# The layer norm of layer 1 by row tiles inside the feed-forward's tail, and modulation columns from one-column products

## What is computed

```
mod = (silu(c) @ wmod).reshape(1, 6, 1, 512)       # wmod is 512 x 3072
sa, ca, ga, sb, cb, gb = mod parts 0..5
g = (2 * (g >= 0) - 1) * maximum(abs(g), 0.25)      # for ga and gb
h = layernorm(x) * (1 + ca) + sa
x = x + ga * attention(h)
h = layernorm(x) * (1 + cb) + sb
x = x + gb * ffn(h)
```

## Time and profile before

| | |
|---|---|
| median of three runs | 1811.9 us |
| the profiled execution | 1815.9 us, its span 1814.0 us |
| busy in the span | PE 92%, its weight loads 74%, DVE 66%, ACT 56%, POOL 40% |
| mean granted clock of TensorE | 0.958 |
| norm 1 and feed-forward of layer 0 | about 979 to 1236 us |
| norm 2 and QKV of layer 1 | about 1236 to 1316 us |
| output of layer 1's attention, norm 3 | about 1681 to 1753 us |

### The profile page before, as it was taken

One profiled execution on the slowest core, in us unless ns is written; L12 is line 12 of the kernel. 1 busy time (PEld: TensorE's weight loads), 2 busy tenths in 40 slices (PEclk: granted clock), 3 DMA queues, 4 the chain that ended last, 5 costly groups with the idle time before them and its releaser, 6 DMA issues. The chain is left out here.

```text
span 1814.0 us, 28444 instructions
## 1 busy us (share of the span) xinstructions
PE 1675.2 (92%) x10115; PEld 1344.5 (74%) x10115; DVE 1192.8 (66%) x2924; ACT 1008.7 (56%) x2229; POOL 724.9 (40%) x656
## 2 busy tenths in 40 slices
PE   4899999999999999999997799996779999999778
PEld 2698999999999999899885588784645555554557
DVE  5667777677677777777667533355876777773475
ACT  2477777777877777777773211102216666666131
POOL 3286675756747567485531200000532222211200
PEclk8999999999999999999999899997959999999889
DMA  7101000000010100100003112005000000000021
GB/s 187 37 13 30 19 24 26 23 30 18 25 36 13 30 19 24 30 13 24 18 7 88 67 53 65 2 1 184 1 1 1 1 1 1 1 1 1 30 45 47
DMA packets 72358, 56.07 MB, mean 31 GB/s; under 512 B 23023, under 2 KB 54447, under 8 KB 72219
## 3 DMA queue, kind: packets, MB, share of 16 engines
q1 hardware_dynamic: 70634, 53.47, 10.2%
q10 hardware_dynamic: 1584, 0.79, 0.2%
HBM read 52.14 MB, written 2.10 MB: 30 GB/s over the span
## 5 line engine op out<-in xcount | busy, mean ns | idle before, releaser
L746 PEld LDWEIGHTS psum<-a_probsT,a_v 128*128 128x128 f32 x2304 | 294.7, 191 | 25.6 <-issue 3.9
L746 PE MATMUL psum<-a_probsT,a_v 128*128 128x128 f32 x2304 | 299.2, 275 | 1.7 <-ACT a_probsT L956 1.6
L845 DVE CUSTOM_DVE_ANT_0 psum<-psum,a_keys_allowed 128x128 f32<-128x128 f32 (+7 forms) x256 | 195.7, 764 | 83.0 <-PE psum L77 74.4
L939 ACT ACTIVATE a_probs<-psum,a_neg_max 128x128 f32<-128x128 f32 (+7 forms) x256 | 190.7, 745 | 66.6 <-DVE a_neg_max L845 58.2
L1827 ACT ACTIVATE a_probsT<-psum 128x512 f32<-128x512 f32 (+3 forms) x384 | 174.6, 497 | 86.4 <-PE psum L1664 62.4
L948 ACT ACTIVATE a_probs<-a_probs,a_row_inv 128x128 f32<-128x128 f32 (+7 forms) x256 | 201.1, 786 | 27.9 <-DVE a_row_inv L852 27.7
L609 POOL TENSOR_TENSOR a_turned_pool<-a_q_sum,a_sine 64x512 f32<-64x512 f32 x62 | 79.3, 1278 | 287.8 <-DVE a_q_sum L831 286.6
L875 DVE TENSOR_TENSOR a_ctxT_lo<-psum,a_ctxT_hi 128x128 fp32r<-128x128 f32 x256 | 73.7, 288 | 172.7 <-ACT a_ctxT_hi L962 172.6
L956 ACT COPY a_probsT<-psum 128x512 f32<-128x512 f32 (+3 forms) x384 | 173.2, 488 | 18.7 <-PE psum L734 16.6
L865 DVE SCALAR_TENSOR_TENSOR a_sumT<-psum,a_scale_o,a_sumT 128x512 f32<-128x512 f32 x248 | 173.6, 742 | 0.9 <-PE psum L760 0.7
L734 PE MATMUL psum<-ident,a_probs 128*128 128x128 f32 x1152 | 168.9, 274 | 0.7 <-ACT a_vT L933 0.5
(11 more groups left out here) (348 smaller groups left out, 3963.7 us busy)
## 6 DMA issues: line engine op xcount, KB each, us to landing
a_raw_o<-in_L_attn_qw_o SPq DMA_DIRECT2D x32, 256.0 KB, 2.8
a_raw_q<-in_L_attn_qw_q SPq DMA_DIRECT2D x31, 256.0 KB, 3.3
mod1b_w<-in_L_wmod SPq DMA_DIRECT2D x4, 1024.0 KB, 11.3
mod0a_w<-in_L_wmod SPq DMA_DIRECT2D x3, 1024.0 KB, 13.0
mod0b_w<-in_L_wmod SPq DMA_DIRECT2D x3, 1024.0 KB, 7.0
f_raw<-in_L_ffn_down_w SPq DMA_DIRECT2D x10, 256.0 KB, 3.1
f_raw<-in_L_ffn_gate_w SPq DMA_DIRECT2D x10, 256.0 KB, 3.3
f_raw<-in_L_ffn_up_w SPq DMA_DIRECT2D x10, 256.0 KB, 3.6
```

What stands on the lines that cost most here:

```text
L746: last = nc.tensor.matmul(bank(use)[:, 0:P], v[:, g % 2, j, :], probsT[:, u % 2, j, :], start=(j == 0), stop=(j == i))
L845: nc.vector.tensor_tensor_reduce(out=scores, in0=scores, in1=keys_allowed[:, S - (i + 1) * P:S], scale=-1.0, scalar=-MASKED, op0=ALU.add, ...
L939: nc.scalar.activation(probs[:, u % 3, 0:(i + 1) * P], score[u % 2][:, 0:(i + 1) * P], ACT.Exp, bias=neg_max[:, h % 2, i:i + 1], scale=-1. ...
```

## The change

It has four parts.

1. **One-column products.** A modulation column is made straight: the stationary is a 128 by 128 block of wmod, the streamed operand one column of silu(c); four blocks of k add into one PSUM column, and 32 such products give two parts. DVE then only copies four numbers per partition and adds 1 to the scale. The diagonals are gone. `silu_rows` is needed only for gate rows; ACT makes it now.
2. **Layer 1's first columns in norm 1.** The two parts of wmod that norm 2 used are loaded in norm 1's block behind the first weight tiles. PE makes their columns at that block's end, DVE takes them.
3. **Norm 2 by row tiles in the feed-forward's tail.** The class `RowNorm` does the whole norm for a single tile: DVE begins (statistics), ACT takes the root, DVE finishes, PE turns four blocks, ACT applies scale and shift in place in PSUM and casts, DVE makes the low part. Its steps stand between those of the down product. The cast of the hidden tile goes from DVE to ACT. Tiles 6 and 7 are completed in the QKV block.
4. **w_qkv in the tail.** It is loaded in four blocks of columns (384 KB each, in pieces of 512 bytes), turned behind the down products of tiles 2 to 5, cast by ACT, and its low part made by DVE. The QKV block begins with its products at once; the bias and the table of the rotation are the first loads in it. Places in on-chip memory are assigned by hand so that all this fits beside the feed-forward.

The core of the diff:

```diff
-    def make_columns(self, pe, pair, silu_rows, rows_used):
-
-        pe.wait_ge(self.mem.modulation["rows_done"], KT * rows_used)
+    def make_columns(self, pe, pair):
+
         for c, n in enumerate(pair):
-            last = self.multiply(pe, n, silu_rows, self.mem.bank[4 + c])
+            pe.wait_ge(self.mem.modulation[f"w_in{n}"], 16 * (self.layer + 1))
+            for piece in range(KT):
+                for k in range(KT):
+                    last = self.nc.tensor.matmul(self.mem.bank[4 + c][:, piece:piece + 1],
+                                                 self.w[:, self.parts.index(n), k, piece * P:(piece + 1) * P],
+                                                 self.mem.silu_c[:, self.layer, k:k + 1], start=(k == 0), stop=(k == KT - 1))
         last.then_inc(self.mem.modulation["column_made"], 1)
 
-    def take_columns(self, dve, pair, diagonals):
+    def take_columns(self, dve, pair):
 
         at = 4 * self.layer + (0 if pair[0] == 0 else 2)
-        number = self.number(pair[0])
-        dve.wait_ge(self.mem.modulation["column_made"], number)
-        for c in range(2):
-            for k in range(KT):
-                self.nc.vector.scalar_tensor_tensor(
-                    out=diagonals[c][:, k * P:(k + 1) * P], in0=self.mem.bank[4 + c][:, k * P:(k + 1) * P], scalar=1.0,
-                    in1=self.mem.ident[:, :], op0=ALU.mult, op1=ALU.mult,
-                    accum_out=self.mem.column[:, at + c, k:k + 1]).then_inc(self.mem.modulation["diagonals"], 1)
-        dve.wait_ge(self.mem.modulation["diagonals"], 2 * KT * number)
-        self.nc.vector.tensor_scalar(self.mem.column[:, at + 1, :], self.mem.column[:, at + 1, :], 1.0, None, ALU.add
+        dve.wait_ge(self.mem.modulation["column_made"], self.number(pair[0]))
+        self.nc.vector.tensor_copy(self.mem.column[:, at, :], self.mem.bank[4][:, 0:KT])
+        self.nc.vector.tensor_scalar(self.mem.column[:, at + 1, :], self.mem.bank[5][:, 0:KT], 1.0, None, ALU.add
...
+            if next_columns:
+                next_columns.take_columns(dve, (0, 1))
 
...
+            if next_columns:
+                modulation.wait_columns(pe, pair)
+                next_columns.make_columns(pe, (0, 1))
...
+    def begin(self, dve, t):
+        nc, sem = self.nc, self.by_dve.sem
+        nc.vector.bn_stats(self.stats[:, t, :], self.mem.x[:, t, :]).then_inc(sem, 1)
+        dve.wait_ge(*self.by_dve.of(("stats", t)))
+        nc.vector.bn_aggr(self.mean_var[:, t, :], self.stats[:, t, :]).then_inc(sem, 1)
+        dve.wait_ge(*self.by_dve.of(("moments", t)))
+        nc.vector.tensor_scalar(self.y[:, t, :], self.mean_var[:, t, 1:2], LN_EPS, None, ALU.add).then_inc(sem, 1)
+
+    def finish(self, dve, t):
+        nc, sem, of = self.nc, self.by_dve.sem, self.by_dve.of
+        root, newton = self.root[:, t, :], self.newton[:, t, :]
+        dve.wait_ge(*self.by_act.of(("std", t)))
+        nc.vector.reciprocal(root, self.std[:, t, :]).then_inc(sem, 1)
+        dve.wait_ge(*of(("root", t)))
+        nc.vector.tensor_tensor(newton, root, root, ALU.mult).then_inc(sem, 1)
+        dve.wait_ge(*of(("square", t)))
+        nc.vector.tensor_tensor(newton, newton, self.y[:, t, :], ALU.mult).then_inc(sem, 1)
+        dve.wait_ge(*of(("product", t)))
+        nc.vector.tensor_scalar(newton, newton, -0.5, 1.5, ALU.mult, ALU.add).then_inc(sem, 1)
+        dve.wait_ge(*of(("newton", t)))
+        nc.vector.tensor_tensor(self.rstd[:, t, :], root, newton, ALU.mult).then_inc(sem, 1)
+        dve.wait_ge(*of(("rstd", t)))
+        if t >= 2:
+            dve.wait_ge(*self.turned.of(t - 2))
+        nc.vector.tensor_scalar(self.normed[:, t % 2, :], self.mem.x[:, t, :], self.mean_var[:, t, 0:1], self.rstd[:, t, :],
+                                ALU.subtract, ALU.mult).then_inc(sem, 1)
+
+    def low(self, dve, t):
+        dve.wait_ge(*self.by_act.of(("high", t)))
+        cols = self.columns(t)
+        self.nc.vector.tensor_tensor(self.mem.hT[1][:, :, cols], self.banks[t % 2].rearrange("p (k n) -> p k n", k=KT),
+                                     self.mem.hT[0][:, :, cols].bitcast(F32), ALU.subtract).then_inc(self.by_dve.sem, 1)
+
...
+    def modulate(self, act, t):
+        act.wait_ge(*self.turned.of(t))
+        bank = self.banks[t % 2]
+        for k in range(KT):
+            piece = bank[:, k * P:(k + 1) * P]
+            last = self.nc.scalar.activation(piece, piece, ACT.Identity, scale=self.scale[:, k:k + 1], bias=self.shift[:, k:k + 1])
+        last.then_inc(self.by_act.sem, 1)
+        act.wait_ge(*self.by_act.of(("h", t)))
+        self.nc.scalar.copy(self.mem.hT[0][:, :, self.columns(t)], bank.rearrange("p (k n) -> p k n", k=KT)
+                            ).then_inc(self.by_act.sem, 1)
+
+    def turn(self, pe, t):
+        pe.wait_ge(*self.by_dve.of(("normed", t)))
+        if t >= 2:
+            pe.wait_ge(*self.by_dve.of(("low", t - 2)))
+        for k in range(KT):
+            last = self.nc.tensor.transpose(self.banks[t % 2][:, k * P:(k + 1) * P], self.normed[:, t % 2, k * P:(k + 1) * P],
+                                            self.mem.ident[:, :])
+        last.then_inc(self.turned.sem, 1)
...
+                if 1 <= t < NT - 1:
+                    norm.turn(pe, t - 1)
+                if 0 <= t - NEXT_FIRST < KT:
+                    turn_next(t - NEXT_FIRST)
...
+            act.wait_ge(*hidden_done.now(LAST, "up"))
+            for t in range(1, NT):
+                if t + 1 < NT:
+                    cast(t + 1)
+                if t >= 2:
+                    norm.modulate(act, t - 2)
+                if 0 <= t - 1 - NEXT_FIRST < KT:
+                    take_next(t - 1 - NEXT_FIRST)
+                norm.deviation(act, t - 1)
...
-            for t in range(NT):
+                dve.wait_ge(added, t + 1)
+
+            def split_next(k):
+                dve.wait_ge(next_hi, k + 1)
+                nc.vector.tensor_tensor(next_wT[1][:, k, :], next_bank, next_wT[0][:, k, :].bitcast(F32), ALU.subtract
+                                        ).then_inc(next_split, 1)
+
+            for t in range(2):
+                split(t, slice(LAST, NF), t + 3)
+            for t in range(1, NT):
+                add(t - 1)
+                if t + 1 < NT:
+                    low_part(t + 1)
+                norm.begin(dve, t - 1)
                 if t >= 2:
-                    dve.wait_ge(produced, t - 1)
-                split(t, slice(LAST, NF) if t < 2 else slice(0, NF), t + 3)
-                if t:
-                    add(t - 1)
-            add(NT - 1)
-
-
-def layer1_qkv_phase(nc, mem, q1, k1, v1, rope_dram, w_dram, b_dram, wmod, late):
+                    norm.low(dve, t - 2)
+                norm.finish(dve, t - 1)
+                if 0 <= t - 1 - NEXT_FIRST < KT:
+                    split_next(t - 1 - NEXT_FIRST)
...
+            norm.turn(pe, NT - 2)
             for t in range(NT):
+                if t == 1:
...
+            dve.wait_ge(produced, NT)
+            nc.vector.tensor_tensor(mem.x[:, NT - 1, :], mem.bank[(NT - 1) % 2][:, :], mem.x[:, NT - 1, :], ALU.add).then_inc(added, 1)
+            dve.wait_ge(added, NT)
+            norm.begin(dve, NT - 1)
+            norm.low(dve, NT - 2)
+            norm.finish(dve, NT - 1)
```

More of the change, by code:

```diff
@@ L1011, in layer0_ffn_phase @@
+def layer0_ffn_phase(nc, mem, w, wmod, wmod_next, w_qkv):
     slots, kts, tiles, halves, matrices = range(2), range(KT), range(NF), range(NHALF), (2, 0, 1)
@@ L1085, in stack_low, with loads_of_next @@
                                    ALU.subtract).then_inc(low_step, 1)
+        def loads_of_next(sp):
+            loads(sp)
+            for n in (0, 1):
+                next_modulation.load(sp, n)
         with ExitStack() as first:
@@ L1196, in _, with turn_next @@
                 project(f, 1, 1)
+            def turn_next(k):
+                pe.wait_ge(next_in[k % 2], 16 * (k // 2 + 1))
+                if k:
+                    pe.wait_ge(next_split, k)
+                for c in range(NC):
+                    last = nc.tensor.transpose(next_bank[:, c * P:(c + 1) * P], next_raw[:, k % 2, c, :], mem.ident[:, :])
+                last.then_inc(next_turned, 1)
             for t in range(NT):
@@ L1338, in loads @@
                 late.load(sp, n)
-        with ExitStack() as first:
-            modulation = Modulation(nc, mem, first, "mod1a", 1, (0, 1), wmod)
-            layernorm_phase(nc, mem, 2, loads, modulation)
-        wT = (sb("wT_hi", [P, KT, QKV1], F32R), sb("wT_lo", [P, KT, QKV1], F32R))
-        qkv = sb("qkv", [P, 2, QKV1])
-        part = [sb(f"part{n}", [P, NH, NP]) for n in range(4)]
-        roped = sb("roped", [P, 2, NH, HD1])
-        wT_turned, w_hi, w_split = sem("wT_turned"), sem("w_hi"), sem("w_split")
-        projected, biased, v_out = sem("projected"), sem("biased"), sem("v_out")
-        turned = {"even": sem("even_turned"), "odd": sem("odd_turned")}
-        summed = {"even": sem("even_summed"), "odd": sem("odd_summed")}
```

(6 more changed lines are left out.)

242 lines of the change are left out of this document (154 added, 88 removed).

## The result

The changed kernel takes 1791.96 us (median of four, 1791.2 to 1792.77) against 1811.91 (1811.73 to 1813.33): ratio 0.9889, 95% interval 0.9872 to 0.9906. Its profiled execution took 1791.9 us, span 1789.8, against 1815.9 and 1814.0: 24.2 us less. The profiled execution before lay 4.0 us above its median, this one lies on it, so some 4 of the 24.2 belong to the executions and not to the change. Timed again beside the kernel before, it was 23.0 us faster (1789.73 against 1812.77).

The account below looks back on a forecast made before the run. PE was taken to bound the feed-forward's tail, a chain the hand-over, and DVE the QKV stage and last norm. -28.9+5.5+2.1 = -21.3 us gave 1790.6 on the median, forecast 1791 us, range 1778 to 1800.

Parts of the forecast that it names:

- A: Feed-forward tail and hand-over to QKV: layer-norm block and w_qkv turning leave the path, transposes join PE's tail; -28.9 us.
- the low part ahead of the second QKV tile: QKV stage: DVE's low part of tile 7 (0.69 us) goes where 0.46 us was idle; 0.5 us back.
- B: Norm before the feed-forward: one-column products and layer 1's columns make it longer; +5.5 us, bounds +2.3 and +8.8.
- C: Last norm (run 3): DVE loses silu copies and diagonals, but columns and gate row come later; +2.1 us, bounds -2.1 and +6.6.
- the middle between full and half clock: Last norm: columns ready at 1736.3 at full clock, 1742.8 at half; 1739.5 was taken.
- Nothing: Norm of run 0 and the output phase's silu rows: no effect, since ACT is held until 31.09 by weight loads.
- 1 (full clock): Rival: one-column products run at full clock since PE counts as busy; -31.5 in all, 1780 us, chance 0.28.
- PE counts as busy: Reason given for full clock in the one-column products: PE counts as busy, so the clock rises.
- the statement on transposes: Skill page, used for the clock in the norm before the feed-forward: transposes don't lift the clock as products do.
- 2 (0.46 us a record): Rival: one-column products adding into one PSUM column wait for each other, 0.46 us a record; +45, 1857 us, chance 0.06.
- 3: Rival: DVE bounds the tail, its round 9.6 instead of 7.5 us, PE waits before six products; 1797 us, chance 0.10.
- 4: Rival: the small bias and rope loads land late, first QKV tile starts at 1250; +4, 1795 us, chance 0.11.

Follow-up runs that it names:

- second profile: The changed kernel timed and profiled again with no edit, on the chip of the follow-up runs: 1789.73 us.
- 32 bytes further: The changed kernel with every hand-placed tensor of the feed-forward moved 32 bytes further, nothing else: 1795.32 us.
- 32 columns: The changed kernel with every column product streaming 32 equal columns of silu(c) instead of one: 1792.65 us.
- address sweep: The changed kernel with 216 unused products added ahead of the tail, their operands starting at different addresses: 1847.29 us in one execution.

## Why the prediction was right, point by point

**A, the hand-over: right, but for one step.** Forecast -28.9, measured -34.2+3.8+0.8 = -29.6. Its terms: block change, four transposes, one product and the way to VectorE come to 5.4 us behind the last product's end, as forecast. The transposes cost 0.115 (groups of four: 7.96-7.50 over 4) and 0.11 us, the upper bound and not the 0.09 of the earlier trace rows, so 5.4 us and not 4.8. That is offset by the down products, 7.50 instead of 7.72 us a tile, 1.8 us in all, which no step of mine had. VectorE's round is 7.0 us (8.63-1.64), 7.5 was estimated; its busy time 5.97 as forecast; ACT's is 4.2 to 4.3, near 4 was. The step that failed is the last one: the low part ahead of the second QKV tile, put at 0.5, costs nothing. The rest of QKV is 0.8 longer because PE waits for the normed rows of tile 7 (0.41 us from its last record to the first transpose, where 0.12 is usual) and then makes their four transposes (0.41) before the second product. These transposes stood in no sum of mine.

**B: right in mechanism, a bit too dear.** Forecast +5.5, measured +3.9 and +2.9 in two profiles, both within the bounds. The first set took 13.8 us, the 13.7 of half clock. But the clock rose 3.9 us into the transposes that follow, so the gate row took 3.6 us and not 5.7, and the second set 9.3 instead of some 10.5; VectorE's gate steps covered all but 0.8 of it. The block became 1.8 us longer, not 5.5. The other 2.1 us are what the sum had not, the clock behind the block: it was back 11.0 us after the feed-forward's start, where the kernel before has it at 6.2. Nine profiles have one-column products there: the clock was back 6.2 us after the feed-forward's start in one, 10.4 to 11.6 in the others.

**C: the size was off.** Forecast +2.1, measured +3.6, and 1.7 less in the second profile, both within the bounds. The step was the middle between full and half clock: columns 10.4 us forecast, 11.0 measured; and the gate row behind them, which I put at the 5.7 us of norm 1, took 6.6 because the clock stayed down through it.

**"Nothing": right.** In norm 0 the columns were ready at 28.4 us, ACT was held until 30.1 by the loads. The 0.9 us gained in attention 0 lie within what the same code does from execution to execution (938.3 to 941.1 us in the other profiles). The stretch ahead of it took 44.6 us in the one profile of the kernel before and 42.9 to 43.9 in all others; whether that 1 us is the change's is not shown.

**Rivals.** 1 (full clock) is wrong: the clock did not rise in 13.8 us of such records, and fell 3.0 us into them in norm 3 and 4.8 in norm 1. The argument for it, "PE counts as busy", is what the experiments refute. But my own argument against it was too wide. I took the transposes of w_qkv for a model of all short work, and 128-column products kept the clock in norm 3 and lifted it in norm 1. Even for transposes it is too wide: in norm 1 the clock rose 3.9 us into them (at 1000.1), behind 13.8 us of one-column products that had not lifted it, and 3.6 to 4.1 us into them in the nine profiles with one-column products there. That is against the statement on transposes which the prediction took from the Trainium skill, and the measurement decides. 2 (0.46 us a record) is wrong, it is 0.112 and 0.213. 3 is wrong, with 1.6 us to spare. 4 is wrong: the bias landed 3.2 us after its issue, and VectorE's first biased tile waited for nothing but its own norm.

The Trainium skill, "TensorE: Matmul & The Clock Gate", section on LDWEIGHTS, has loading go by the stationary's columns whatever streams; the trace agrees at full clock (0.112 us a record with 1, 32 and 128 columns) and not at half (0.213). By it alone the width would not matter, and from 1 to 128 columns it was worth 5.7 us in norm 3.

That the forecast met the median to 1 us is in part luck. B was 1.6 us too high and C 1.5 too low. A, B and C together measure -22.1 us in the two profiles, where -21.3 was forecast, while the medians differ by 19.95 us in the result and by 23.0 when both were timed again.

## What to carry to other kernels

A product that costs only its weight load can stream 128 columns for the same price, and here that was worth 5.7 us in one norm, since it kept the clock for what came behind. Old columns behind the new tail (1784.42 us) and 128 columns (1785.1, 1782.62) are all faster than the changed kernel: a part that has a price of its own wants a run of its own. Price a short product at half clock unless a row shows it at full, and price the work behind it too. When an expected difference shows, look for the place of it: one here had the right size and the wrong reason.

## What the hardware showed beyond that

The clock can fall behind a gap of 2 us in an otherwise full PE: in two of the profiles (32 bytes further, and 32 columns) it fell for 3.4 us, 1.2 and 1.4 us after such a gap ahead of the tail, and this made 67.0 and 66.9 us of 65.3. In the address sweep it did so 1.5 us after a gap of 2.4. In the other profiles the same gap of 2 us is there and the clock did not fall. And the same down products stood 3% closer after the change at the same clock, 0.227 instead of 0.234 us; shifts by 32 and 64 bytes leave it, and what sets it is open.
